# Half-height one-hots on two quarters of TensorE, and two of four banks summed on VectorE, in a three-layer GNN

## The chip, the cores and the metric

The kernel runs on one core of one Trainium2 chip. The metric is the device time of one execution in microseconds, the median over runs. All lines (L1404 and the like) are lines of the kernel before.

## The reference, cut to what matters

```python
h = jnp.maximum(_layernorm(x, axis=-1), 0.0)         # x: (12500, 64) fp32
for l in range(3):
    mlp = lambda z: jnp.maximum(z @ W1[l] + b1[l], 0.0) @ W2[l] + b2[l]
    msgs = mlp(h[dst])                               # 400,000 edges
    agg = segment_sum(msgs, src, num_segments=12500)
    h = mlp(h + agg)
return x + (h @ Wf + bf)
```

The edges are sorted by `dst`. Several edges may join the same two nodes.

## The kernel before, in words

**The idea.** Every layer sums the messages of the `dst` nodes into the `src` nodes over the same edges. So the kernel first builds a matrix of counts, "how many edges lead from this dst node to that src node", four bits a count, in DRAM (`counts_dram`). Each layer is then a dense product: message parts (`parts`, two fp16 halves that add up to the fp32 value) times unpacked counts (read as fp8), added up in PSUM. Layer 0 is in part multiplied while the matrix is still being built.

**Windows.** The nodes are handled as 49 tiles (`WT`) of 128 pairs of neighbouring dst nodes. The edges of a pair lie in one stretch of the sorted list. In the setup TensorE (L1336) and ScalarE (L1113, an activation with a sum) find for every pair where its stretch starts, in units of 16 edges (`GRAN`), in seven batches of seven tiles, and VectorE (L715 to L717) makes them the addresses `start_i`. The packing of edges into words (row key, column key, weight) is VectorE's L701 to L709 with a cast by GpSimd (L610). Per tile one indirect DMA of GpSimd (L621, `gather`) fetches 128 edges for each of the 128 pairs; six tiles are in flight (`WR`). ScalarE splits a tile's words (L1130, L1131), TensorE turns them so that edges lie on partitions (L1347, L1349), and ScalarE copies them to SBUF (`keep_keys`, L1139 to L1143).

**One-hots and the build.** A tile is done in four groups (`HG`) of 32 pairs. The loop over the 196 groups `k` is written out by hand on every engine, and each engine runs through its own list in order:
- VectorE's `make_hots(k)` compares keys with a row of numbers (both L754). Column one-hots `hot_c`: 26 two-byte words per pair, which hold 52 fp8 columns. Row one-hots `hot_r`: 128 per pair, 64 for each of its two dst nodes. From group 32 on ScalarE makes two of the 32 row one-hots (`find_few_distances` L1167, `make_few_rows` L1173), so that VectorE makes 30 (3840 elements). There are two slots: group k waits until the matmuls of group k-2 are done.
- GpSimd's `weigh(k)` (L636) multiplies the column one-hots by each edge's weight, as 416 words of 32 bits.
- TensorE's `multiply_group(k)` (L1375): one matmul per pair, all 128 edges by 128 rows (two nodes of 64) by 53 columns; the last column counts the edges. The result lies in two PSUM slots of 16 pairs.
- ScalarE's `keep_batch` (L1182, L1184) copies it out, VectorE's `turn_counts(k-2)` transposes it (L762), and SyncE stores it (L453).

**The rounds.** From tile 8 (`AHEAD`) on, TensorE does a part of layer 0 in every group, behind the build matmuls: `add_bank(u, b)`, with one unit `u` per tile and one bank `b` of four per group. A unit is 448 columns of a seventh of the nodes (`SB` = 7 stretches) and two chunks of seven tiles, so 14 matmuls of 448 columns (L1404). Seven units make a round over all stretches. From the second round on (unit 7, tile 15) the sums so far are first put back into the bank by a product with the identity in fp32 (`add_kept`, L1399), and after the 14 matmuls ScalarE copies the bank out again (`keep_sums`, L1191). Two banks of PSUM serve in turn. VectorE unpacks the counts for it, one pass a group (`unpack_low` L794, `unpack_high` L802), and makes `parts` where due (L843). SyncE loads the counts (L464).

The order on VectorE in group k, quoted in short, with L754, L762 and L794 or L802 in it:

```python
make_hots(k)                                   # columns, then rows
if k >= LAG: turn_counts(k - LAG)
if h == 0 and u >= 0: unpack_low(ROUND * u + 1)
if h == 1 and u >= 0: unpack_high(ROUND * u)
if h == 2 and u >= 0: unpack_high(ROUND * u + 1)
if h == 3 and 0 <= unit_of(j + 1) < FUSED: unpack_low(ROUND * unit_of(j + 1))
```

**Behind the build** eight units are left, then layers 1 and 2 (L1525, with the small matmuls L1481, L1487 and L1503 of the node network between the chunks).

## Time and profile before

| | |
|---|---|
| median of 3 runs | 2164.39 us (2163.72 to 2164.80) |
| the profiled execution | 2161.14 us |
| its span | 2159.4 us, mean granted clock of TensorE 0.979 |
| TensorE busy | 2025.7 us (94%), 15741 matmuls |
| VectorE busy | 1454.3 us (67%) |
| ScalarE busy | 793.6 us (37%) |
| GpSimd busy | 609.3 us (28%) |

The busy share of TensorE counts matmuls whose ends are modelled, so that neighbours overlap by a little; the distance from one start to the next is what a stream costs. The span falls into a setup (to 57.7 us), the build without rounds (to 194 us), the build with rounds (to 922 us), and the rest, in which TensorE has hardly any idle time. The page's slices show VectorE at nine tenths or more from slice 2 to slice 17 of 40, and at three to six tenths after them.

### The profile page before, as it was taken

What the parts mean: (1) busy time and instruction counts of PE and PEld (TensorE: products, weight loads), DVE (VectorE), ACT (ScalarE), POOL (GpSimd) and SP (SyncE); (2) the same over time, 40 slices, a digit from 0 to 9 for tenths busy, and PEclk for the clock granted to TensorE, in tenths of its full rate; (3) what the DMA queues carried; (4) which work ended last, traced back from release to release, by engine and by line L of the source; (5) the groups of instructions that cost most, each with busy time, mean ns of one, the idle gap of its engine ahead of it and who ended that gap; (6) DMA issues with size and microseconds to landing.
All of it is one profiled execution on the core that took longest, in us unless ns stands there. A gap on an engine that the chain in (4) does not pass through costs nothing.

```text
span 2159.4 us, 39820 instructions
## 1 busy us (share of the span) xinstructions
PE 2025.7 (94%) x15741; PEld 1138.4 (53%) x15741; DVE 1454.3 (67%) x1656; ACT 793.6 (37%) x2228; POOL 609.3 (28%) x273
## 2 busy tenths in 40 slices
PE   4565889999999999999999999999999999999998
PEld 3444445555565555555555555555555555555554
DVE  7999999999999999946643343343365444434433
ACT  4996887777777778722200000000010000000000
POOL 3666666666767666600000000000000000000000
PEclk8796999999999999999999999999999999999999
DMA  7356666666666666653444543543543555555452
GB/s 201 75 137 186 178 170 207 189 200 197 193 194 193 189 191 188 190 175 90 150 149 120 164 146 107 164 149 111 172 149 113 179 160 154 159 159 159 142 164 71
DMA packets 332829, 344.51 MB, mean 160 GB/s; under 512 B 21562, under 2 KB 303992, under 8 KB 332184
## 3 DMA queue, kind: packets, MB, share of 16 engines
q1 hardware_dynamic: 327516, 335.59, 52.6%
q0 software_dynamic: 2352, 6.43, 1.1%
q8 instruction: 94, 1.54, 0.3%
q10 hardware_dynamic: 2816, 0.53, 0.2%
q14 instruction: 51, 0.42, 0.1%
HBM read 252.58 MB, written 89.89 MB: 159 GB/s over the span
## 4 chain that ended last, share of the span: by engine, by line
PE 75%; DVE 15%; issue 3%; DMA 3%; ACT 2%; POOL 1%; SPq 1%; DVEq 0%; POOLq 0%; ACTq 0%
PE ps L1525 48%; PE ps L1404 15%; DVE arena L754 7%; PE ps L1375 4%; PE ps L1399 4%; DVE arena L762 3%; DMA arena<-counts_dram 2%; PE ps L1481 2%; PE ps L1503 1%; POOL arena L636 1%; PE ps L1487 1%; DVE arena L802 1%; SPq L453 1%; DVE arena L794 1%; ACT arena L1182 1%
## 5 line engine op out<-in xcount | busy, mean ns | idle before, releaser
L1525 PE MATMUL ps<-arena,parts 128*128 128x448 fp8e4 x5488 | 1049.1, 353 | 0.8 <-DVE arena L890 0.8
L1525 PEld LDWEIGHTS ps<-arena,parts 128*128 128x128 f16 x5488 | 534.7, 98 | 514.2 <-issue 24.6
L636 POOL TENSOR_TENSOR arena<-arena,weight_now 128x416 int32<-128x416 int32 x196 | 518.3, 2644 | 273.6 <-DVE arena L754 271.3
L877 DVE TENSOR_SCALAR arena<-arena 128x3136 uint16<-128x3136 uint16 x196 | 191.4, 976 | 592.2 <-PE ps L1525 592.2
L1404 PE MATMUL ps<-arena,parts 128*128 128x448 fp8e4 x2744 | 550.8, 353 | 1.5 <-DVE parts L843 1.5
L754 DVE TENSOR_TENSOR arena<-row_iota,key_now 128x3840 f16<-128x3840 f16 (+1 forms) x196 | 425.8, 2172 | 0.0
L1404 PEld LDWEIGHTS ps<-arena,parts 128*128 128x128 f16 x2744 | 266.4, 98 | 291.2 <-issue 73.1
L1274 ACT ACTIVATE arena<-arena 128x448 f32<-128x448 f32 x42 | 24.2, 577 | 988.9 <-DVE arena L904 988.9
L1182 ACT ACTIVATE arena<-ps 128x800 uint16<-128x800 f32 x392 | 338.4, 872 | 31.4 <-PE ps L1375 31.0
L1375 PE MATMUL ps<-arena 128*128 128x53 fp8e4 x6272 | 205.3, 189 | 76.6 <-POOL arena L636 64.1
L1375 PEld LDWEIGHTS ps<-arena 128*128 128x128 f16 x6272 | 195.6, 98 | 125.3 <-DVE arena L754 76.7
L762 DVE STREAM_TRANSPOSE arena<-arena 128x800 int32<-128x800 int32 x196 | 196.7, 1004 | 3.4 <-DMA counts_dram<-arena 3.4
L878 DVE TENSOR_SCALAR arena<-arena 128x3136 uint16<-128x3136 uint16 x196 | 190.2, 970 | 0.0
L627 POOL PARTITION_ALL_REDUCE scal<-scal x2 | 2.0, 1014 | 649.8 <-DVE scal L822 649.8
L649 POOL PARTITION_ALL_REDUCE good<-good x1 | 0.4, 409 | 565.4 <-DVE good L1031 565.4
L754 DVE TENSOR_TENSOR arena<-word_iota,key_now 128x832 uint16<-128x832 f16 x196 | 114.9, 586 | 0.0
L1167 ACT ACTIVATE few_far<-row_iota,few_now 128x128 f16<-128x128 f16 x328 | 112.1, 393 | 0.0
L794 DVE TENSOR_SCALAR arena<-arena 128x3136 uint16<-128x3136 uint16 x82 | 77.2, 942 | 5.0 <-DMA arena<-counts_dram 4.9
L621 POOL DMA_INDIRECT arena<-edges_dram,start_i x49 | 76.5, 1561 | 8.0 <-issue 5.4
L802 DVE TENSOR_SCALAR arena<-arena 128x3136 uint16<-128x3136 uint16 x82 | 76.6, 934 | 0.0
L1184 ACT ACTIVATE row_edges<-ps 128x16 f16<-128x16 f32 x392 | 75.6, 193 | 0.0
L1399 PE MATMUL ps<-msg,ident 128*128 128x448 f32 x140 | 68.9, 573 | 2.7 <-DVE arena L862 2.7
(150 smaller groups left out, 1176.7 us busy)
## 6 DMA issues: line engine op xcount, KB each, us to landing
arena<-counts_dram SPq DMA_DIRECT2D x294, 784.0 KB, 4.6
counts_dram<-arena SPq DMA_DIRECT2D x784, 100.0 KB, 2.2
h_dram<-parts SPq DMA_DIRECT2D x2, 1536.0 KB, 7.2
edges_dram<-arena SPq DMA_DIRECT2D x2, 1400.0 KB
arena<-in_x_dram SPq DMA_DIRECT2D x14, 192.0 KB
out_dram<-arena SPq DMA_DIRECT2D x14, 192.0 KB
arena<-in_dst_dram SPq DMA_DIRECT2D x1, 1400.0 KB
arena<-in_src_dram SPq DMA_DIRECT2D x1, 1400.0 KB
```

The source lines that it names most:

```text
L636: nc.gpsimd.tensor_tensor(pairs, pairs, weight_now[:, h * HW:(h + 1) * HW].unsqueeze(2).to_broadcast([P, HW, WORDS // 2]), ALU.mult).then_ ...
L754: return v.tensor_tensor(out, numbers.rearrange("p (m two) -> p m two", two=2).unsqueeze(1).to_broadcast(shape), key.unsqueeze(2).to_broad ...
L762: v.transpose(ctile[:, k % 2, :].bitcast(I32), stage[:, k % 2, :].bitcast(I32)).then_inc(s["counts_turned"], 1)
L794: v.tensor_scalar(spread[:, n % WIDE, 0, :].bitcast(U16), ring0[:, n % RING0, :].bitcast(U16), 0x0F0F, None, ALU.bitwise_and).then_inc(s[" ...
L877: v.tensor_scalar(spread[:, c % WIDE, 0, :].bitcast(U16), packed, 0x0F0F, None, ALU.bitwise_and)
L878: v.tensor_scalar(spread[:, c % WIDE, 1, :].bitcast(U16), packed, 4, 0x0F0F, ALU.logical_shift_right, ALU.bitwise_and).then_inc(s["counts_ ...
L1167: last = a.activation(few_far[:, c, :], row_iota[:], ACT.Abs, bias=few_now[:, k % HG, c:c + 1])
L1182: a.activation(to, product(q)[:, :, 0:2 * LP].rearrange("p c (m two) -> p c m two", two=2), ACT.Copy, scale=1.0 / WEIGHT_UNIT)
L1375: last = t.matmul(product(q)[:, c, 0:COLS], hot_r[:, slot, w, :], hot_c8[:, slot, w, 0:COLS], start=True, stop=True)
L1399: t.matmul(ps[:, bank, 0:NB], ident[:], kept_sums(u % SB, b), start=True, stop=False)
L1404: last = t.matmul(ps[:, bank, 0:NB], parts[:, (ROUND * (u // SB) + c) * CK + k, :], spread[:, c, b // 2, at:at + NB].bitcast(F8), start=(u ...
L1525: last = t.matmul(ps[:, b, 0:NB], parts[:, c * CK + k, :], spread[:, c % WIDE, b // 2, at:at + NB].bitcast(F8), start=start, stop=stop)
```

## The change

- A pair's two nodes get windows of their own: the partitions 0 to 63 hold 64 edges from the start of the first node, 64 to 127 hold 64 edges of the second (`REACH` = 64). The unit of a start is 8 edges instead of 16. There are two indirect DMAs per tile, of half the size each.
- The row one-hots of a pair are 64 wide instead of 128 (2048 elements per group), all on VectorE; ScalarE's part (L1141, L1167, L1173) goes.
- The column one-hots are fp16 instead of fp8: 50 words per pair instead of 26, and GpSimd multiplies 800 words of 32 bits.
- A pair takes two matmuls of 64 edges by 64 rows by 51 columns, on the quarters (rows 0 to 63, columns 0 to 63) and (64 to 127, 64 to 127) of the array.
- From unit 7 on, two of the four banks (`ADDED` = 0 and 2) are no longer put back by TensorE; VectorE adds the bank to the kept sums (`add_sums`), in the next group, between the transpose and the unpacking.
- The starts of 20 tiles are found in the setup, in five batches of four, with fp16 steps in two parts; those of the other 29 in the build, one tile each, seven tiles ahead (`node_step` and `find_starts` on VectorE, `make_fan_now` on TensorE, `count_fan_now` on ScalarE).
- The packing has fewer passes on VectorE; GpSimd's cast becomes a multiply and add. A small DMA of the next 64 entries of `dst` is put ahead of the load of `src` on SyncE's queue.

The diff, cut to its core:

```diff
-GRAN = 16
+GRAN = 8
+REACH = WIN // 2
+BATCH = 4
+BATCHES = 5
+FANS = BATCH * BATCHES
+FAN_AHEAD = 7
-FEW = 2
-FEW_FROM = 32
+ROWS = HROWS * HI
-WORDS = 2 * 13
+WORDS = 2 * LP
-COLS = 2 * WORDS + 1
+COLS = WORDS + 1
+ADDED = (0, 2)
...
-        hot_r, at = view(0, [SLOTS, HW, P], F16)
-        hot_c, at = view(at, [SLOTS, HW, CPITCH], F16)
+        hot_r, at = view(0, [SLOTS, HW, ROWS], F16)
+        hot_m, at = view(at, [SLOTS, HW, CPITCH], F16)
...
+        def sums_freed(u, b):
+            if u >= SB and b in ADDED:
+                return s["sums_added"], len(ADDED) * (u - SB) + ADDED.index(b) + 1
+            left = [n for n in range(SBB) if n not in ADDED]
+            if u >= SB:
+                return s["sums_kept"], SBB * SB + len(left) * (u - SB) + left.index(b) + 1
+            return s["sums_kept"], SBB * u + b + 1
...
@@ gpsimd, gather(t)
-                pool.indirect_dma_start(win[:, t % WR, :], None, edges_dram.rearrange("(r f) -> r f", f=2 * GRAN),
-                                        bass.IndirectOffsetOnAxis(ap=start_i[:, t:t + 1], axis=0)).then_inc(
-                    windows_gathered[t % WR], 16)
+                for d in range(2):
+                    pool.indirect_dma_start(win[:, t % WR, d * WIN:(d + 1) * WIN], None,
+                                            edges_dram.rearrange("(r f) -> r f", f=2 * GRAN),
+                                            bass.IndirectOffsetOnAxis(ap=start_i[:, t, d:d + 1], axis=0)).then_inc(
+                        windows_gathered[t % WR], 16)
@@ gpsimd, weigh(k)
-                pairs = hot_c[:, k % SLOTS, :, 0:WORDS].bitcast(I32)
+                pairs = hot_m[:, k % SLOTS, :, 0:WORDS].bitcast(I32)
@@ vector, packing of the edges, per half
-                v.tensor_scalar(e1[:, c], src_t[:, c], 3, None, ALU.bitwise_and)
-                link(v.tensor_scalar(e2[:, c], src_t[:, c], 4, None, ALU.bitwise_and), dve)
-                link(v.tensor_scalar(e2[:, c].bitcast(F32), e2[:, c], 32.0 * 255 / 4, 32.0, ALU.mult, ALU.add), dve)
+                link(v.tensor_scalar(e1[:, c], src_t[:, c], 3, None, ALU.bitwise_and), dve)
...
-                v.scalar_tensor_tensor(pk_weight[:, units, :], by_units(e1)[:, units, :], 0.25,
-                                       by_units(e2.bitcast(F32))[:, units, :], ALU.add, ALU.mult).then_inc(s["edges_packed"], 1)
+                v.tensor_scalar(pk_weight[:, units, :], by_units(e1)[:, units, :], 4096.0, 15360.0, ALU.mult,
+                                ALU.add).then_inc(s["edges_packed"], 1)
@@ vector, make_hots(k)
-                few = FEW if k >= FEW_FROM else 0
-                compare_keys(hot_r[:, slot, few:HW, :].rearrange("p c (m two) -> p c m two", two=2), row_iota[:], P,
-                             key_now[:, u, 0, w.start + few:w.stop, :]).then_inc(s["rows_made"], 1)
+                compare_keys(hot_r[:, slot, :, :].rearrange("p c (m two) -> p c m two", two=2), row_iota[:], ROWS,
+                             key_now[:, u, 0, w, :]).then_inc(s["rows_made"], 1)
@@ vector
+            def add_sums(u, b, bank):
+                dve.wait_ge(s["sums_done"], SBB * u + b + 1)
+                dve.wait_ge(*sums_freed(u - SB, b))
+                kept = kept_sums(u % SB, b)
+                v.scalar_tensor_tensor(kept, ps[:, bank, 0:NB], scal[:, 0, 6:7], kept, ALU.mult, ALU.add).then_inc(
+                    s["sums_added"], 1)
@@ vector, in the loop over k, behind turn_counts
+                before = unit_of((k - 1) // HG)
+                if before >= SB and (k - 1) % HG in ADDED:
+                    add_sums(before, (k - 1) % HG, (k - 1) % 2)
@@ vector, in the loop over k, behind the unpacking
+                if fan_of(j) >= 0 and h == 0:
+                    node_step(fan_of(j))
+                if fan_of(j) >= 0 and h == 3:
+                    find_starts(fan_of(j), 1)
@@ scalar, setup: per tile two passes of 408 in place of one of 200
+            def count_fan(t, frm, scrap):
+                for d in range(2):
+                    a.activation(scrap[:, d, :], frm[:, 0:FANX], ACT.Sign, scale=-1.0, bias=node_less[:, d, t:t + 1],
+                                 accum_out=signs[:, t, d:d + 1])
@@ scalar, in the loop over k
-                if k and unit_of((k - 1) // HG) >= 0:
-                    b = (k - 1) % HG
-                    keep_sums(unit_of((k - 1) // HG), b, b % 2)
-                if FEW_FROM <= k + 1 < BUILD * HG:
-                    find_few_distances(k + 1)
+                before = unit_of((k - 1) // HG)
+                if before >= 0 and ((k - 1) % HG not in ADDED or before < SB):
+                    keep_sums(before, (k - 1) % HG, (k - 1) % 2)
...
+                if fan_of(j) >= 0 and h == 2:
+                    count_fan_now(fan_of(j))
@@ tensor, multiply_group(k)
-                        last = t.matmul(product(q)[:, c, 0:COLS], hot_r[:, slot, w, :], hot_c8[:, slot, w, 0:COLS], start=True,
-                                        stop=True)
+                        for d in (slice(0, REACH), slice(REACH, WIN)):
+                            last = t.matmul(product(q)[d, c, 0:COLS], hot_r[d, slot, w, :], hot_m[d, slot, w, 0:COLS],
+                                            start=True, stop=True)
@@ tensor, add_bank(u, b)
-                    pe.wait_ge(s["sums_kept"], SBB * u + b - 1)
+                    pe.wait_ge(*sums_freed(*divmod(SBB * u + b - 2, SBB)))
...
-                if u >= SB:
+                if u >= SB and b not in ADDED:
+                    pe.wait_ge(*sums_freed(u - SB, b))
                     add_kept(u, b, b % 2)
@@ tensor, in the loop over k
+                if h == 1 and fan_of(j) >= 0:
+                    make_fan_now(fan_of(j))
```

## Rows read from the trace of the kernel before

**Rows 1.** The page, the chain that ended last, by line
```profile
PE ps L1525 48%; PE ps L1404 15%; DVE arena L754 7%; PE ps L1375 4%; PE ps L1399 4%; DVE arena L762 3%; DMA arena<-counts_dram 2%; PE ps L1481 2%; PE ps L1503 1%; POOL arena L636 1%; PE ps L1487 1%; DVE arena L802 1%; SPq L453 1%; DVE arena L794 1%; ACT arena L1182 1%
```

**Rows 2.** Windows over L754: us, busy DVE (instructions), clock, DMA share, GB/s
```profile
57.60:194.40 136.80, 89.87 (x64) 0.77 0.49 126
194.40:326.70 132.30, 74.21 (x56) 0.96 0.63 182
326.70:918.40 591.70, 357.76 (x270) 1.00 0.66 193
```

**Rows 3.** Timeline of one group: start us, us, engine, line, what [idle before]
```profile
602.51 1.71 POOL L621 DMA_INDIRECT arena<-edges_dram,start_i  x1
...
602.81 1.00 PE L1375 MATMUL ps<-arena 128*128 128x53 fp8e4 x32
...
603.30 0.57 DVE L754 TENSOR_TENSOR arena<-word_iota,key_now 128x832 uint16<-128x832 f16 x1
...
603.64 1.00 PE L1399 MATMUL ps<-arena,ident 128*128 128x448 f32 x2
603.81 2.14 DVE L754 TENSOR_TENSOR arena<-row_iota,key_now 128x3840 f16<-128x3840 f16 x1
...
604.24 2.48 POOL L636 TENSOR_TENSOR arena<-arena,weight_now 128x416 int32<-128x416 int32 x1
...
604.48 2.81 PE L1404 MATMUL ps<-arena,parts 128*128 128x448 fp8e4 x14
...
605.88 0.99 DVE L762 STREAM_TRANSPOSE arena<-arena 128x800 int32<-128x800 int32 x1
606.80 0.92 DVE L794 TENSOR_SCALAR arena<-arena 128x3136 uint16<-128x3136 uint16 x1
...
607.13 1.00 PE L1375 MATMUL ps<-arena 128*128 128x53 fp8e4 x32
...
607.66 0.57 DVE L754 TENSOR_TENSOR arena<-word_iota,key_now 128x832 uint16<-128x832 f16 x1
```

**Rows 4.** Timeline, the first group of the build, VectorE and GpSimd
```profile
58.18 2.29 DVE L754 TENSOR_TENSOR arena<-row_iota,key_now 128x4096 f16<-128x4096 f16 x1
58.42 2.81 POOL L636 TENSOR_TENSOR arena<-arena,weight_now 128x416 int32<-128x416 int32 x1 [5.40 <-DVE arena L754]
60.38 1.29 DVE L754 TENSOR_TENSOR arena<-word_iota,key_now 128x832 uint16<-128x832 f16 x1
```

**Rows 5.** Lines by form: row one-hots; busy us, mean ns, idle before
```profile
L754 DVE TENSOR_TENSOR arena<-row_iota,key_now 128x3840 f16<-128x3840 f16 x164 | 352.7, 2151 | 0.0
...
L754 DVE TENSOR_TENSOR arena<-row_iota,key_now 128x4096 f16<-128x4096 f16 x32 | 73.0, 2282 | 0.0
```

**Rows 6.** Lines by form: a bank read with one kept operand
```profile
L890 DVE SCALAR_TENSOR_TENSOR arena<-ps,scal,msg 128x448 f32<-128x448 f32 x14 | 9.5, 681 | 3.9 <-PE ps L1404 3.9
```

**Rows 7.** Lines by form: fp32 weight loads of 128 and of 64 columns
```profile
L1487 PEld LDWEIGHTS ps<-arena,W1b 128*128 128x128 f32 x56 | 10.6, 190 | 6.5 <-issue 5.2
...
L1481 PEld LDWEIGHTS ps<-arena,W1s 128*64 128x64 f32 x168 | 8.8, 135 | 16.4 <-issue 15.8 <-DVE arena L893 0.7
```

**Rows 8.** Timeline of TensorE in a later layer
```profile
1052.44 0.97 PE L1481 MATMUL ps<-arena,W1s 128*64 128x448 f32 x4
1053.35 5.47 PE L1525 MATMUL ps<-arena,parts 128*128 128x448 fp8e4 x28
...
1064.96 1.67 PE L1487 MATMUL ps<-arena,W1b 128*128 128x448 f32 x4
1066.46 10.76 PE L1525 MATMUL ps<-arena,parts 128*128 128x448 fp8e4 x56
```

**Rows 9.** Timeline of VectorE in the setup, one small link
```profile
38.74 0.17 DVE L717 TENSOR_SCALAR start_i<-start_f 128x7 int32<-128x7 f32 x1
```

**Rows 10.** Lines by form: setup on ScalarE and VectorE
```profile
L1113 ACT ACTIVATE row_edges<-ps,node_less 128x200 f16<-128x200 f32 x49 | 20.4, 465 | 1.2 <-PE ps L1336 1.2
...
L709 DVE SCALAR_TENSOR_TENSOR arena<-arena 125x1600 f16<-125x1600 int32 x2 | 3.6, 1818 | 0.0
```

More of the change, by code:

```diff
@@ L695, in _ @@
+            for n in range(BATCHES):
                 node_steps(n)
@@ L722, in _ @@
+            for n in range(2):
+                find_starts(n * BATCH, BATCH)
             less, var, inv, tmp = (stat[:, j, :] for j in range(4))
@@ L728, in _ @@
                 if t.start == 0:
-                    for n in range(3, 5):
-                        find_starts(n)
+                    for n in range(2, 4):
+                        find_starts(n * BATCH, BATCH)
             link(last, dve)
@@ L738, in _ @@
             v.tensor_tensor(less, counted[:, 1, 0, :], counted[:, 1, 1, :], ALU.add)
-            for n in range(5, GROUPS):
-                find_starts(n)
+            for n in range(4, BATCHES):
+                find_starts(n * BATCH, BATCH)
             dve.wait_ge(s["root_made"], 1)
@@ L1264, in _ @@
                     keep_weights()
-            keep_sums(FUSED - 1, SBB - 1, (SBB - 1) % 2)
-            for b in range(SBB):
-                keep_sums(FUSED, b, b)
+            for u, b in [(FUSED - 1, SBB - 1)] + [(FUSED, b) for b in range(SBB)]:
+                if b not in ADDED:
+                    keep_sums(u, b, b if u == FUSED else b % 2)
             def epilogue(l, i):
@@ L1326, in _, with make_fan @@
             pe.wait_ge(s["shift_made"], 1)
-            pe.wait_ge(s["firsts_made"], 1)
-            t.matmul(ps[0:EP, 0, 0:FAN], shift, firsts, start=True, stop=True).then_inc(s["firsts_shifted"], 1)
+            pe.wait_ge(s["lasts_made"], 1)
+            t.matmul(ps[0:EP, 0, 0:FANX + 1], shift, lasts[:, 0:FANX + 1], start=True, stop=True).then_inc(s["lasts_shifted"], 1)
             pe.wait_ge(s["rises_made"], 1)
-            for n in range(GROUPS):
+            def make_fan(to, steps):
+                for part in range(2):
+                    last = t.matmul(to, steps, rises[:, part, 0:FANX + 1], start=part == 0, stop=part == 1)
+                return last
+            for n in range(BATCHES):
                 pe.wait_ge(s["steps_made"], n + 1)
```

245 lines of the change are left out of this document (139 added, 106 removed).

## The prediction

> **What bounds the kernel now.** I read the chain that ended last first, for the lines that set the end. It gives 48% to the matmuls of the later layers (L1525), 15% to those of the build's rounds (L1404), and 7% to the one-hots of VectorE (L754) [rows 1]. The change leaves L1525 alone, so the question is the build, whose stages the windows over L754 show [rows 2]: 32 groups (64 one-hots, two per group) in 136.8 us before the rounds begin, 28 in 132.3 us in the rounds that add nothing kept, 135 in 591.7 us after them, or 4.38 us a group. That last stage decides.
>
> One group in order of time [rows 3] shows two engines full at once. **VectorE**, start to start: column one-hots 0.51, row one-hots 2.07, transpose 0.92, unpack 0.86; 4.36 us. **TensorE**: 32 build matmuls 0.83, the kept sum brought back as fp32 0.84, 14 matmuls of the round 2.65; 4.32 us. A third resource hides in the same rows. GpSimd's multiplication (L636) starts at 604.24, 0.43 into VectorE's row one-hots, and ends at 606.72, 0.77 after they end (605.95), inside the transpose. That looks like a wait, not like work. In the one place without a transpose behind [rows 4] the row one-hots end at 60.47 and GpSimd's end is 61.23; the next column one-hots, 0.58 us long with nothing in their way, take 1.29. So each of the two holds the other up: the multiplication itself is 0.71 to 0.76 us, say 0.72, of exclusive time for 416 elements, and the transpose hides it.
>
> **The change, part by part** (136 groups from tile 15 on, in pairs, since every second bank is treated another way).
>
> *VectorE's one-hots.* Rows go from 3840 to 2048 elements. 4096 against 3840 elements is 2282 against 2151 ns [rows 5], 0.51 ns each, so 2.07 becomes 1.15. Columns go from 832 to 1600 elements of the same two bytes: 0.51 becomes 0.90. Together 2.58 becomes 2.05.
>
> *GpSimd's multiplication* grows from 416 to 800 elements. In proportion to 0.72 that is 1.38 us of exclusive time [rows 4]; below, it could be as little as 0.72, were it all fixed, and above I see no row. I take 1.38, as no fixed part shows. The transpose (0.92) no longer covers it, so VectorE waits 0.46 for its unpack, unless an add stands there too.
>
> *The adds on VectorE.* Two banks of four become a read of a bank with one kept operand, the form of L890, 0.68 us long [rows 6], 0.60 start to start. A group with one: 2.05 + 0.92 + 0.60 + 0.86 = 4.43. One without: 2.05 + 1.38 + 0.86 = 4.29. This alone is 8.72 a pair against 8.76 now: what the one-hots save, the lock and the adds take back. But an add also waits for its bank. The multiplication of group k ends 3.43 after the group began on VectorE and 0.17 pass until a load; then come X (the build matmuls), 2.65, 0.16 for the last matmul's end (2.81 in place of 2.65 [rows 3]), the add 0.60 and the unpack 0.86 before group k+2 can start: 7.9 + X a pair.
>
> *TensorE.* Two kept sums of four go: 0.84 less in a pair. The 32 build matmuls of 128 rows by 53 columns become 64 of 64 rows by 51 columns, on two opposite quarters. This is X, and no row shows it. From below: both quarters work at once and a pair costs what one costs now, 0.83 us a group. From above: a load of 64 columns and its matmul per quarter, one after another. Loads of 64 and 128 fp32 columns are 135 and 190 ns [rows 7]; 55 ns for 64 columns, times 64, is 3.5 us. In the middle: the present rate, one load and matmul in 26 ns (0.83 / 32), is a rate of issue, and 64 give 1.67; or both quarters load at once at 55 ns, 32 x 55 = 1.76. Two of my routes meet there, so I take 1.67. Going to another division of the array and back costs too: four passes of L1481 on two halves take 0.91 to the next matmul, four of L1487 on the whole array 1.50 [rows 8]. At full overlap the former would be 0.75, so the two changes cost 0.16, and they come in every group: X = 1.83.
> The Trainium skill (TensorEngine Tiling (Array Packing), Key Properties) says that tiles load and multiply in parallel and that changing the mode drains the engine; the L1481 rows agree with both, for 448 columns.
> The Trainium skill (TensorE: Matmul & The Clock Gate, Weight-path perf modes and LDWEIGHTS) speaks against the change: the fast load needs all 128 columns and goes off with column tiling, and a plain load costs the columns over 1.2 GHz, 53 ns for 64. By that X is 1.7 if the loads overlap and 3.4 if they don't.
>
> A pair on TensorE is then 2 x (1.83 + 2.65) + 0.84 = 9.80, and VectorE's loop 7.9 + 1.83 = 9.73. TensorE leads. A tile of four groups adds about 0.17 for turning keys, which lay beside VectorE before: 19.8.
>
> *Fans in the rounds.* 29 of 49 tiles (20 to 48) get their window starts in the build, in tiles 13 to 41. TensorE: two matmuls of 409 columns, near 2.65 / 14 = 0.19 each, 0.35 a tile with loads. VectorE: three small links of 0.17 [rows 9] and a step, 0.65 a tile. ScalarE: about 1.5 us in a tile, covered, as it loses the near-row helpers (L1167, L1173) and half of the kept copies. So tiles 15 to 41 take 20.15 against 17.53 (4 x 4.38): 27 x 2.62 = +71. Tiles 42 to 48: 7 x 2.27 = +16.
>
> *Tiles 8 to 14.* TensorE 1.83 + 2.65 + 0.04 = 4.52, VectorE 4.29 and 0.6 for parts in every second group, as before: 0. ScalarE keeps all banks here.
>
> *Before the rounds.* A group is 2.05 + 1.38 = 3.43, against 3.63 (0.51 + 2.20 [rows 4] + 0.92); where a message follows (13 groups), it runs in GpSimd's time and saves the 0.46 more. That is -12. GpSimd issues a second gather per tile: 1.71 [rows 3], so two outlast the 2.1 free before its next multiplication by about 1 us in eight tiles, +8. If the multiplication then misses its gap it waits a whole one-hot, which I count in the range.
>
> *Setup.* VectorE drops two passes over 1600 elements in each half and its 1.82 us pass L709 [rows 10] has one source; at half of 1.82 for a one-source pass, 2 x 2.7 = -5. ScalarE's counting: 40 passes of 408 in place of 49 of 200, 465 ns each [rows 10]; 20 us becomes some 24, beside the stores of the edges. The load of dst's next 64 entries stands ahead of src on SP's queue, at well under 1 us. Twelve gathers against six, at most 1.71 each, come ahead of the first multiplication; they start earlier by what the packing saves. I take -5 for all. The drain behind the build loses two kept sums: -1.
>
> **Sum**: +71 + 16 + 0 - 4 - 5 - 1 = +77 on the profiled execution's 2161.1, which is 2238; the median of the runs is 3.3 above it, 2241.5. Everything behind the build is untouched.
>
> **Rivals.**
> *Quarters at once* (X = 0.99 with the mode changes). For it: L1481 ran its halves together. Against: those matmuls are eight times as long as these, so issue never showed. VectorE's loop then leads: 8.9 a pair and 0.5 a tile, 18.3 against 17.53: +21 in tiles 15 to 41, +2 behind, -2 in tiles 8 to 14, -10 before: 2176. Slower in spite of it.
> *Faster: the lock is cheap.* X = 0.99, and GpSimd's multiplication is mostly fixed cost, so that the transpose still covers it. It decides on the unpack's start behind the transpose: below 0.92 us of exclusive time VectorE pays nothing. A pair is then 3.83 + 4.43 = 8.26 and its loop 8.4, so tiles 15 to 41 17.3 (-6), 42 to 48 16.8 (-5), tiles 8 to 14 28 x 0.5 (-13), before them -13, setup and end -6: 2121, and between that and 2176 for a lock between 0.92 and 1.38.
> *Loads one after another*, X = 3.66: a pair on TensorE 13.5, a tile 27.5: +270 and +68, +46 in tiles 8 to 14, +30 before: 2565. For it: nothing in the trace shows two loads together. Against: nothing shows them held apart. The Trainium skill's rule on the fast load, without overlap, gives the same.
> *The change does nothing*: excluded, since the shapes change on every engine.
>
> **Numbers.** Forecast 0.42, quarters at once 0.25, faster 0.20, loads in turn 0.13. The range leaves out the loads in turn and the low end of the faster case: 2125 to 2275, which takes X from 0.9 to 2.0. A measurement of this kernel tells about 0.2% (4.3 us) from no change. Faster 0.22 (0.02 from the quarters case), same 0.06, slower 0.72.
>
> **What would show it.** Right: in the rounds TensorE without idle time, 64 build matmuls in 1.6 to 1.9 us, groups of 4.9 to 5.1 us; VectorE waiting for L1404 ahead of its adds; L636 still ending in or just behind the transpose, now with 1.4 us behind the row one-hots. Wrong: build matmuls of a group under 1.2 us (then read VectorE's unpack: late by 0.46 or not), or over 2.5 us; an L636 that ends 0.9 us or less behind the row one-hots; a setup that moves by over 10 us.

## The result, and the profile after

The changed kernel (span of the profiled execution 2209.8 us) takes **2214.8 us** (median, 2211.7 to 2215.8) against 2164.6 in the same call: ratio **1.0227, 95% interval 1.0209 to 1.0244**, 50 us slower. The forecast was 2241.5. Direction and range held; the size was 27 us too large, on a forecast excess of 77.

First the page, its chain that ended last, by engine and by line.

```profile
PE 88%; issue 4%; DVE 3%; ACT 2%; DMA 2%; POOL 1%; SPq 0%; DVEq 0%; POOLq 0%; ACTq 0%
PE ps L1618 47%; PE ps L1494 24%; PE ps L1465 9%; PE ps L1489 3%; PE ps L1574 2%; PE ps L1596 1%; DVE arena L822 1%; PE ps L1580 1%; DMA arena<-in_src_dram 1%; POOL arena L674 1%; POOL arena L690 1%; ACT parts L1218 1%; ACT arena L1260 1%; PE ps L1409 0%; DMA edges_dram<-arena 0%
```

L1618 is the old L1525, L1494 the old L1404, L1465 the build matmul (old L1375), L1489 the kept sum (old L1399) [rows 1]. VectorE's one-hots have left the chain (7% to 1%), and it looks as if TensorE bounded the build. It doesn't, as the timeline shows. Next the stages, windows over the one-hots (L822, old L754), which answer to [rows 2]; columns as there.

```profile
54.40:193.60 139.20, 74.64 (x65) 0.77 0.50 127
193.60:324.00 130.40, 59.22 (x57) 0.96 0.66 189
324.00:965.70 641.70, 285.94 (x271) 1.00 0.63 178
```

The 50 us lie in the last row, 641.7 us in place of 591.7. The first group starts 3.2 us earlier, groups 0 to 31 take 2.4 more, tiles 8 to 14 1.9 less. Within the last row, tiles 15 to 41, which now also make window starts, go from 17.55 to 19.19 us each (27 tiles, +44), and the groups of tiles 42 to 48 from 4.37 to 4.57 (+6). What is behind the last group grew by 3 us. That is not TensorE's work: the rounds that are left end 1.5 us sooner than before, and the layers behind them take the same. 4.4 us stand at the very end, from VectorE's last operation to the end of the span (4.7 us before, 9.0 now), where GpSimd's last instruction, a drain, takes 8.15 us in place of 4.07. All the changed kernels have it (8.6 to 9.0 us); why is not shown.

Now the timeline of the changed kernel over one of the tiles with a fan, VectorE, TensorE and GpSimd only (start, us, engine, line, operation, and in brackets the idle time before it). It starts with the third group of a tile.

```profile
601.72 0.98 DVE L822 TENSOR_TENSOR arena<-word_iota,key_now 128x1600 uint16<-128x1600 f16 x1
...
602.17 0.52 PE L1409 MATMUL ps<-arena 125*128 125x409 f16 x2
...
602.52 0.92 PE L1489 MATMUL ps<-msg,ident 128*128 128x448 f32 x2
602.62 1.22 DVE L822 TENSOR_TENSOR arena<-row_iota,key_now 128x2048 f16<-128x2048 f16 x1
602.85 2.39 POOL L690 TENSOR_TENSOR arena<-arena,weight_now 128x800 int32<-128x800 int32 x1 [2.08 <-DVE arena L822]
...
603.27 2.81 PE L1494 MATMUL ps<-arena,parts 128*128 128x448 fp8e4 x14
...
603.75 1.00 DVE L830 STREAM_TRANSPOSE arena<-arena 128x800 int32<-128x800 int32 x1
604.68 1.39 DVE L869 TENSOR_SCALAR arena<-arena 128x3136 uint16<-128x3136 uint16 x1
...
606.01 1.19 PE L1465 MATMUL ps<-arena 64*64 64x51 f16 x64
...
608.94 1.55 POOL L690 TENSOR_TENSOR arena<-arena,weight_now 128x800 int32<-128x800 int32 x1
610.00 0.68 DVE L1042 SCALAR_TENSOR_TENSOR arena<-ps,scal,arena 128x448 f32<-128x448 f32 x1 [0.97 <-PE ps L1494]
...
610.60 0.97 DVE L861 TENSOR_SCALAR arena<-arena 128x3136 uint16<-128x3136 uint16 x1
...
611.95 0.99 DVE L822 TENSOR_TENSOR arena<-word_iota,key_now 128x1600 uint16<-128x1600 f16 x1
...
613.09 2.39 POOL L690 TENSOR_TENSOR arena<-arena,weight_now 128x800 int32<-128x800 int32 x1 [2.60 <-DVE arena L822]
...
615.58 1.19 PE L1465 MATMUL ps<-arena 64*64 64x51 f16 x64 [0.20 <-issue]
...
616.71 2.82 PE L1494 MATMUL ps<-arena,parts 128*128 128x448 fp8e4 x14
...
619.57 0.68 DVE L1042 SCALAR_TENSOR_TENSOR msg<-ps,scal,msg 128x448 f32<-128x448 f32 x1
...
621.05 0.98 DVE L822 TENSOR_TENSOR arena<-word_iota,key_now 128x1600 uint16<-128x1600 f16 x1
```

Four readings.

**X is 1.13 us**: from the build matmuls at 615.58 to the round at 616.71, not 1.83.

**The lock is as forecast** (the lock: GpSimd's multiplication and VectorE's operations hold each other up, and what they can't share is the multiplication's exclusive time). The row one-hots end at 603.84, GpSimd's multiplication at 605.24, 1.40 later (forecast 1.38). The transpose covers 0.93 of it and the unpack L869 lasts 1.39 in place of some 0.97.

**A loop leads, not TensorE.** A pair of groups is 9.10 us where nothing comes between. The one that starts at 611.95 ends at 621.05: multiplication's end 3.53, build 0.10 later, X 1.13, round and its last end 2.86, add 0.60, unpack 0.88, in all 9.10. TensorE idles before the build (0.20 there; 0.63 before the one at 610.59). The trace puts that down to "issue", but the build at 615.58 starts 0.10 behind the multiplication's end at 615.48: it is GpSimd's product that it waits for.

**The other pair takes 10.23** (601.72 to 611.95), 1.13 more: find_starts adds 0.47 on VectorE before the next group, and the build at 606.01 starts 0.77 behind the multiplication instead of 0.10, as TensorE is still in the round of 603.27, which came late behind keys turned, the fan (L1409) and a kept sum. 9.10 + 10.23 = 19.33 for this tile, against the stage's mean of 19.19. Over tiles 15 to 41 the two pairs take 9.10 and 10.09 on average, and the build of a tile's third group starts 0.63 behind its multiplication, that of the other three 0.10.

So I had three causes to test: that the quarters work at once, the loop through the add, and the lock. The question behind them is which of these the 50 us are.

### The profile page after: what moved, and what is told of

Its sections match the earlier page's. It is cut to its first block, busy times and chain, and to the rows that moved or that the text cites. A ratio compares the mean times of both kernels' runs of the same rounds, so it can differ in the third digit from the quotient of the medians.

```text
span 2209.8 us, 51883 instructions
## 1 busy us (share of the span) xinstructions
PE 2048.1 (93%) x21873; PEld 1148.9 (52%) x21873; DVE 1454.7 (66%) x1835; ACT 660.3 (30%) x1693; POOL 587.2 (27%) x326
## 4 chain that ended last, share of the span: by engine, by line
PE 88%; issue 4%; DVE 3%; ACT 2%; DMA 2%; POOL 1%; SPq 0%; DVEq 0%; POOLq 0%; ACTq 0%
PE ps L1618 47%; PE ps L1494 24%; PE ps L1465 9%; PE ps L1489 3%; PE ps L1574 2%; PE ps L1596 1%; DVE arena L822 1%; PE ps L1580 1%; DMA arena<-in_src_dram 1%; POOL arena L674 1%; POOL arena L690 1%; ACT parts L1218 1%; ACT arena L1260 1%; PE ps L1409 0%; DMA edges_dram<-arena 0%
## 5 line engine op out<-in xcount | busy, mean ns | idle before, releaser
L1618 PE MATMUL ps<-arena,parts 128*128 128x448 fp8e4 x5488 | 1049.1, 353 | 1.1 <-DVE arena L957 1.1
L1618 PEld LDWEIGHTS ps<-arena,parts 128*128 128x128 f16 x5488 | 534.7, 98 | 514.5 <-issue 24.9
L944 DVE TENSOR_SCALAR arena<-arena 128x3136 uint16<-128x3136 uint16 x196 | 191.3, 976 | 592.4 <-PE ps L1618 592.4
L1494 PE MATMUL ps<-arena,parts 128*128 128x448 fp8e4 x2744 | 552.3, 354 | 2.6 <-issue 2.5
L690 POOL TENSOR_TENSOR arena<-arena,weight_now 128x800 int32<-128x800 int32 x196 | 431.5, 2202 | 327.6 <-DVE arena L822 326.9
L1494 PEld LDWEIGHTS ps<-arena,parts 128*128 128x128 f16 x2744 | 260.9, 98 | 264.6 <-issue 45.0
L1465 PE MATMUL ps<-arena 64*64 64x51 f16 x12544 | 245.8, 191 | 100.1 <-issue 66.1
L1465 PEld LDWEIGHTS ps<-arena 64*64 64x64 f16 x12544 | 228.5, 113 | 176.0 <-issue 175.3
L822 DVE TENSOR_TENSOR arena<-row_iota,key_now 128x2048 f16<-128x2048 f16 x196 | 238.0, 1214 | 0.0
L822 DVE TENSOR_TENSOR arena<-word_iota,key_now 128x1600 uint16<-128x1600 f16 x196 | 199.5, 1018 | 5.9 <-PE ps L1465 5.9
L945 DVE TENSOR_SCALAR arena<-arena 128x3136 uint16<-128x3136 uint16 x196 | 190.0, 970 | 0.0
L674 POOL DMA_INDIRECT arena<-edges_dram,start_i x98 | 143.0, 1459 | 22.9 <-issue 11.1
L861 DVE TENSOR_SCALAR arena<-arena 128x3136 uint16<-128x3136 uint16 x82 | 99.8, 1217 | 2.8 <-DMA arena<-counts_dram 2.8
L869 DVE TENSOR_SCALAR arena<-arena 128x3136 uint16<-128x3136 uint16 x82 | 99.4, 1212 | 0.0
L1302 ACT ACTIVATE parts<-msg,scal 128x448 f16<-128x448 f32 x42 | 25.8, 668 | 100.6 <-DVE msg L982 57.0
L960 DVE TENSOR_SCALAR arena<-ps,scal 128x448 f32<-128x448 f32 x56 | 38.1, 682 | 24.8 <-PE ps L1618 24.6
```

The costliest lines, as they stand in the source:

```text
L674: pool.indirect_dma_start(win[:, t % WR, d * WIN:(d + 1) * WIN], None, edges_dram.rearrange("(r f) -> r f", f=2 * GRAN), bass.IndirectOffs ...
L690: nc.gpsimd.tensor_tensor(pairs, pairs, weight_now[:, h * HW:(h + 1) * HW].unsqueeze(2).to_broadcast([P, HW, WORDS // 2]), ALU.mult).then_ ...
L822: return v.tensor_tensor(out, numbers.rearrange("p (m two) -> p m two", two=2).unsqueeze(1).to_broadcast(shape), key.unsqueeze(2).to_broad ...
L861: v.tensor_scalar(spread[:, n % WIDE, 0, :].bitcast(U16), ring0[:, n % RING0, :].bitcast(U16), 0x0F0F, None, ALU.bitwise_and).then_inc(s[" ...
L869: v.tensor_scalar(spread[:, n % WIDE, 1, :].bitcast(U16), ring0[:, n % RING0, :].bitcast(U16), 4, 0x0F0F, ALU.logical_shift_right, ALU.bit ...
L944: v.tensor_scalar(spread[:, c % WIDE, 0, :].bitcast(U16), packed, 0x0F0F, None, ALU.bitwise_and)
```

## Experiments

All times are medians; the kernel before was run beside each set (2164.7, 2165.7 and 2164.0 in the three sets). "Tile" is the mean of tiles 15 to 41, "group" that of tiles 42 to 48, between starts of the column one-hots. Stages are those of the profiled execution. Ratios are to the kernel before, with 95% intervals.

| kernel | us | ratio | groups 0–31 | tiles 8–14 | tile | group |
|---|---|---|---|---|---|---|
| before | 2164.6 | 1 | 136.7 | 132.3 | 17.55 | 4.37 |
| after | 2214.8 | 1.0227 [1.0209, 1.0244] | 139.2 | 130.4 | 19.19 | 4.57 |
| quarters in turn | 2291.7 | 1.0591 [1.0569, 1.0612] | 160.1 | 134.4 | 20.72 | 5.01 |
| no adds | 2222.5 | 1.0271 [1.0253, 1.0289] | 137.7 | 131.1 | 19.26 | 4.64 |
| half weighed | 2172.9 | 1.0033 [1.0020, 1.0047] | 137.2 | 125.5 | 18.22 | 4.35 |
| late adds | 2208.1 | 1.0207 [1.0190, 1.0225] | 142.1 | 131.1 | 19.02 | 4.38 |
| split gathers | 2220.3 | 1.0252 [1.0235, 1.0269] | 140.7 | 129.6 | 19.44 | 4.55 |
| late adds, split gathers | 2179.4 | 1.0064 [1.0047, 1.0081] | 139.2 | 129.8 | 18.13 | 4.34 |
| late adds, split gathers, starts first | 2199.0 | 1.0155 [1.0138, 1.0172] | 141.9 | 129.8 | 18.85 | 4.34 |
| late, split, starts first, half weighed | 2169.7 | 1.0021 [1.0009, 1.0032] | 136.6 | 121.1 | 18.11 | 4.26 |
| late, split, half weighed | 2157.5 | 0.9968 [0.9956, 0.9980] | 134.4 | 123.6 | 17.82 | 4.30 |
| late, split, gaps used | 2175.5 | 1.0046 [1.0034, 1.0058] | 141.2 | 129.4 | 17.98 | 4.36 |
| late, split, four added | 2184.5 | 1.0094 [1.0079, 1.0109] | 138.1 | 129.7 | 18.40 | 4.41 |

### Do the quarters work at once?

```diff
-                    for c in range(QW):
-                        w = q % 2 * QW + c
-                        for d in (slice(0, REACH), slice(REACH, WIN)):
+                    for d in (slice(0, REACH), slice(REACH, WIN)):
+                        for c in range(QW):
+                            w = q % 2 * QW + c
```

The same 64 matmuls, but 16 on one quarter and then 16 on the other.

> Same 64 build matmuls of a group, but 16 on one quarter, then 16 on the other, and again, instead of alternating. In the changed kernel 64 take 1.13 us to the next matmul, mode changes of 0.16 us included: 15 ns each. If this rate comes from two quarters working at once, in turn each needs 30 ns or more: 2.1 us a group or above, the loop 10.0 us a pair: 2275 us or more (with loads of 53 ns that nothing overlaps, 3.5 us a group and 2450 us). If it is a rate of issue of 15 ns each, nothing changes: 2210 to 2220 us.

Measured 2291.7. The timeline of this kernel:

```profile
955.00 2.82 PE L1494 MATMUL ps<-arena,parts 128*128 128x448 fp8e4 x14
...
957.75 1.90 PE L1465 MATMUL ps<-arena 64*64 64x51 f16 x64
959.59 0.23 PE L1438 MATMUL ps<-ident,rk_now 128*128 128x128 f16 x1
```

In turn the 64 take 1.84 us, alternating 1.13. The starts of the single matmuls in the two traces say more than these sums. In turn they are 27 ns apart on average; alternating 16, two on opposite quarters 3 to 4 ns apart and then 28 to 29 to the next two. From the last of the 64 to the next matmul it is 0.12 us in both kernels, against 0.03 before the change. So alternating quarters overlap, though not fully: 1.7 times the rate, not 2. One quarter alone keeps about the rate of the whole array before (26 ns).

The changes of division come out of the same starts: 0.09 us behind the build, and 0.09 ahead of it (2.75 from the round at 955.00 to the build at 957.75, 2.65 before). That is 0.19 a group, for which the forecast had 0.16, but only half of it lies in X.

Early on, in a stretch of granted clock 0.50 (the 1.2 GHz level), X is 2.95 (63.08 to 66.03) in turn against 1.84 (62.45 to 64.29). And 1.84 at the full clock is my X of 1.83: this kernel is the one that I had forecast, with tiles of 20.72 and groups of 5.01 where I said 20.15 and 4.95. It takes 2291.7, though, and not 2241.5. With its own X the forecast is 50 us too low and out of its range: 27 of them in groups 0 to 31 (+23 us where I said -4), 15 in tiles 15 to 41.

### Is it the adds, or the lock?

```diff
-ADDED = (0, 2)
+ADDED = ()
```

> ADDED is empty: TensorE puts every bank back and ScalarE copies every bank out, as before the change; one-hots, quarters, gathers and fans stay. Theory L: no add, no loop; TensorE leads with 2 x (1.13 + 2.65 + 0.84) = 9.25 us a pair and 19.1 us a tile, without idle time: about the same time as the changed kernel, 2213 us (2205 to 2222). Rival P (TensorE already the bound at 19.2 us a tile): 0.84 more in each pair, 2272 us. Rival G (only VectorE with GpSimd's exclusive time counts): 17.9 us a tile, 2170 us.

Measured 2222.5, just above the range expected: without the adds it is 8 us slower still, with groups of 4.64 where the sum of TensorE's own work said 4.62. By stages, the rounds of tiles 15 to 48 take 3 us more (645.1 for 641.7) and what is behind the last group 7, where TensorE still puts back kept sums that VectorE added before (13 matmuls of L1489 for 6). The adds as such are not the loss; VectorE's adds cost no more than the kept sums that TensorE is spared.

```diff
-                pairs = hot_m[:, k % SLOTS, :, 0:WORDS].bitcast(I32)
+                pairs = hot_m[:, k % SLOTS, :, 0:24].bitcast(I32)
```

(the weight's broadcast is cut to 12 in the same way)

> GpSimd multiplies 384 of the 800 words of a group; the other columns keep their one-hots unweighted, so this part of the counts is left out. Theory L with an exclusive multiplication (1.38 us for 800 words, 0.66 for 384): the unpack behind the transpose is 0.97 us again in place of 1.39, the multiplication ends 0.7 us earlier, a pair's loop falls from 9.0 to 8.3, TensorE leads with 17.4 us a tile: 2145 us (2135 to 2165). Rival P: no change, 2210 to 2218. If the multiplication were mostly fixed cost, it would end at the same distance behind the row one-hots (1.4 us) and the time stay at 2215.

Measured 2172.9, 42 us back, short of the 2145 expected (2135 to 2165). Lines of the last stage for this kernel (its first three rows), then for the changed kernel.

```profile
L690 POOL TENSOR_TENSOR arena<-arena,weight_now 128x384 int32<-128x384 int32 x135 | 205.4, 1522 | 294.1 <-DVE arena L822 234.1 <-ACT weight_now L1237 59.6
...
L869 DVE TENSOR_SCALAR arena<-arena 128x3136 uint16<-128x3136 uint16 x68 | 64.6, 950 | 0.0
L861 DVE TENSOR_SCALAR arena<-arena 128x3136 uint16<-128x3136 uint16 x66 | 63.0, 954 | 3.4 <-DMA arena<-counts_dram 3.3
```

```profile
L690 POOL TENSOR_TENSOR arena<-arena,weight_now 128x800 int32<-128x800 int32 x135 | 299.2, 2216 | 239.8 <-DVE arena L822 239.3
...
L869 DVE TENSOR_SCALAR arena<-arena 128x3136 uint16<-128x3136 uint16 x68 | 80.0, 1177 | 0.0
```

The multiplication now ends 0.71 us behind the row one-hots (603.75 against 603.04), and the unpack, 950 instead of 1177 ns, waits for nothing. From 384 to 800 elements the exclusive time goes from 0.71 to 1.40 us: 1.66 ns for each further element, and hardly a fixed part (1.66 x 384 is 0.64 of the 0.71). That was the assumption of the forecast. But the multiplication stands in the loop as well, so this run shortens both, and can't tell them apart. The next ones can.

### Taking the loop away

```diff
-                before = unit_of((k - 1) // HG)
-                if before >= SB and (k - 1) % HG in ADDED:
-                    add_sums(before, (k - 1) % HG, (k - 1) % 2)
+                before = unit_of((k - 2) // HG)
+                if before >= SB and (k - 2) % HG in ADDED:
+                    add_sums(before, (k - 2) % HG, (k - 2) % 2)
```

VectorE adds a bank one group later, when its round is long done (the last one moves behind the loop).

> VectorE adds the bank of group k-2 instead of k-1, at the same place of its list, so that the bank has long been finished. Reference is the changed kernel: 2214.8 us, 19.2 us a tile in tiles 15 to 41, 4.57 us a group behind them. Theory L (a loop: one-hots, multiplication, build, round, add, unpack, two groups long, 7.9 + 1.13 = 9.0 us a pair and more where TensorE is late): the wait of the adds for L1494 goes, VectorE and the exclusive time of GpSimd are left, 18.2 us a tile and 4.36 us a group: 2182 us (2175 to 2190). Rival P (TensorE's issue of 128 small instructions in a group is the bound, as the chain with 88% TensorE has it): no change, 2210 to 2218.

Measured 2208.1, outside the range expected (2175 to 2190). The groups of tiles 42 to 48 do what the loop theory says, 4.38 from 4.57. The tiles hardly move, 19.02. The timeline of this kernel tells why.

```profile
606.81 1.65 POOL L674 DMA_INDIRECT arena<-edges_dram,start_i  x1 [0.16 <-issue]
...
608.45 1.22 DVE L822 TENSOR_TENSOR arena<-row_iota,key_now 128x2048 f16<-128x2048 f16 x1
...
608.77 1.71 POOL L674 DMA_INDIRECT arena<-edges_dram,start_i  x1 [0.30 <-DVE arena L822]
...
610.50 1.55 POOL L690 TENSOR_TENSOR arena<-arena,weight_now 128x800 int32<-128x800 int32 x1
610.51 2.38 DVE L861 TENSOR_SCALAR arena<-arena 128x3136 uint16<-128x3136 uint16 x1
```

The change issues two gathers in a row. The second ends at 610.48, while the column one-hots that the multiplication waits for were done when the row one-hots began, at 608.45. The multiplication starts at 610.50 in place of some 608.7, loses the time of the transpose, and the unpack pays for it: 2.38 us instead of 1.39. In the changed kernel the same two gathers stand at 605.39 and 607.21 and delay it to 608.94, but there VectorE waits for its bank until 610.00 anyway. With the loop gone the next wait came up. So I issued one gather behind each of two multiplications:

```diff
-                for d in range(2):
+                for d in halves_of:
...
-                if k % HG == 2 and k // HG + WR < WT:
-                    gather(k // HG + WR)
+                if k % HG in (0, 2) and k // HG + WR < WT:
+                    gather(k // HG + WR, (k % HG // 2,))
```

> The late adds, and the two gathers of a tile apart: one behind the multiplication of the tile's first group, one behind that of its third. With late adds alone the third and fourth group took 4.4 and 5.7 us: two gathers of 1.7 us end 0.8 us after the row one-hots, the multiplication comes late, and the unpack (2.38 us in place of 0.97) is held up for its whole length. If that is what the late adds alone left over, the long unpack goes and a tile takes 17.44 + 0.75 = 18.2 us: 2180 us (2172 to 2188). Rival: the gathers cost nothing, the 0.8 us of a tile are fans and turning of keys on TensorE: 2205 to 2210.

> The changed kernel with the gathers apart, adds where the change has them. Theory L: in the rounds the loop over the add's wait leads whether the gathers are early or not (in the tile read, VectorE stands 0.97 us before its add while TensorE finishes L1494): at most 0.2 us a tile, and a few us before the rounds: 2208 us (2203 to 2215). Rival: the gathers alone make the changed kernel slow, 2180 us.

Both edits together: 2179.4, as expected, 35 us of the 50 back. The gathers alone: 2220.3, above the 2208 expected (2203 to 2215). That is no gain; the 5.5 us more than in the changed kernel are hardly clear of the spread (the two intervals overlap). As long as the loop leads, the late multiplication is free. Late adds alone gave 7, so the two are worth 35 only as a pair.

### What is left: VectorE, and the lock

With both edits VectorE runs without waiting for TensorE (group starts at 600.57, 604.85, 609.25, 613.99 and 618.60). Each group is its own work plus the lock. With GpSimd's work halved on top:

> Late adds and split gathers as in the run at 2179, and GpSimd multiplies 384 of the 800 words of a group's column one-hots, so that 416 words a group keep no weight (the output is that of other weights); the start rows are found where they were, so nothing waits for ScalarE's sum. Lock theory: VectorE's unpack no longer waits for GpSimd (0.42 us in groups without an add). The early groups go as in the other half-weigh runs, 2.6 us less in groups 0 to 31 and 8.7 in groups 32 to 59; in the rounds VectorE drops below TensorE, which then leads at 4.26 us a group (tiles 42 to 48 of the run that had both) plus some 0.65 a fan tile, 17.7 against 18.13 us a tile, 11.6 over 27 tiles, and 2.2 in tiles 42 to 48: 2179 - 25 = 2154 us (2145 to 2163). Rival, that the lock costs nothing once nothing waits elsewhere: 2174 to 2182.

Measured 2157.5: 22 us less, and 0.3% faster than the kernel before, though with the output of other weights. Windows over L822 of this kernel, to be read against the ones of the changed kernel:

```profile
53.92:188.35 134.43, 67.21 (x65) 0.80 0.51 132
188.35:311.94 123.59, 59.26 (x57) 0.97 0.67 193
311.94:909.30 597.36, 285.53 (x271) 1.00 0.66 192
```

As late adds and split gathers alone give 139.2, 129.8 and 606.9 us there, halving GpSimd's work gives back 4.8, 6.2 and 9.5. Two groups of a tile without an add pay 0.42 of lock each, 23 us over tiles 15 to 41, and only 8 of them come back there. The groups show why: a tile's second group falls from 4.28 to 3.82, but the first and third, which issue a gather, grow by 0.23 each.

```profile
600.78 0.64 DVE L1042 SCALAR_TENSOR_TENSOR arena<-ps,scal,arena 128x448 f32<-128x448 f32 x1
600.79 0.97 POOL L674 DMA_INDIRECT arena<-edges_dram,start_i  x1
601.34 1.20 DVE L861 TENSOR_SCALAR arena<-arena 128x3136 uint16<-128x3136 uint16 x1
```

The multiplication ends sooner, so that the gather now starts ahead of the unpack and holds it up, 1.20 us instead of 0.96; with the whole multiplication it started behind the unpack and waited itself (1.65 us instead of 0.97). So a gather takes part in the lock too. In tiles 42 to 48, without gathers, TensorE leads: 2 x (1.13 + 2.74) + 0.84 = 8.58 a pair, 4.29 a group, measured 4.30. The 22 us can't be had for the real output, whose 800 elements all need their weight.

The other side of the same claim: where an add stands between transpose and unpack, it should cost only what it exceeds the wait by. All four banks added:

```diff
-ADDED = (0, 2)
+ADDED = (0, 1, 2, 3)
```

> All of the computation; late adds and split gathers as in the run at 2179, and VectorE adds up all four banks instead of two. The add (0.60 us) stands between the transpose and the unpack, where the unpack otherwise waits 0.42 us for GpSimd's weighing. Lock theory: an add in these groups costs 0.60 - 0.42 = 0.14 to 0.18 us in place of 0.60, and 68 such groups from tile 15 on give 10 to 12 us: 2179 + 11 = 2190 us (2183 to 2195). If the wait for GpSimd isn't what the gap is, the add costs its 0.60 in full: 2179 + 41 = 2220 us. TensorE loses a kept matmul in these groups, so it doesn't come up.

Measured 2184.5, the group 4.41 for 4.34 and the tile 18.40 for 18.13. Half of the groups get an add that they hadn't, so it costs them 0.14 us each and not 0.60 (from its start to the unpack's it is 0.56 here, less the wait of 0.42). The gap behind the transpose is GpSimd's.

### Filling the gap

If that gap is idle anyway, the small operations of the fan could stand in it. The first try put find_starts ahead of the unpack in the last group of the tile, with and without the halved multiplication.

> Late adds, gathers apart, and the three links of find_starts ahead of the unpack, in the time in which GpSimd holds VectorE up anyway (0.46 us). A tile 17.7 us in tiles 15 to 41, as before the change (17.55); with 4.38 us a group behind and a few us more in setup and drain: 2167 us (2160 to 2175), the same as before within 0.3%. Rival: the links don't fit there (they need ScalarE's sum of the group before): 2180 us.

> The same with 384 of 800 words multiplied, which leaves the weights of the other columns out. What is left is VectorE's own work, 2 x 3.84 + 2 x 4.44 + 0.5 = 17.1 us a tile, and TensorE's, 4 x 3.78 + 1.69 + 0.6 = 17.4: 2145 us (2135 to 2155), clearly below the kernel before. If instead the exclusive time of GpSimd doesn't count once adds and gathers are out of the way, the same as the run without it, 2167.

Measured 2199.0 and 2169.7, where 2167 and 2145 were expected: both worse than without the move (2179.4 and 2157.5). The timeline of the former:

```profile
605.14 1.00 DVE L830 STREAM_TRANSPOSE arena<-arena 128x800 int32<-128x800 int32 x1
607.27 0.16 DVE L781 SCALAR_TENSOR_TENSOR start_f<-signs,rows_before 128x2 f32<-128x2 f32 x1 [1.14 <-ACT rows_before L1213]
```

VectorE waits 1.14 us for ScalarE's counts, which were ready in time one unpack later. The second try takes them from the tile before, in its second group, makes the fan's step in the fourth group ahead of the unpack, and puts the gathers behind groups 1 and 3:

```diff
+                if h == 1 and fan_of(j - 1) >= 0:
+                    find_starts(fan_of(j - 1), 1)
+                if h == 3 and fan_of(j + 1) >= 0:
+                    node_step(fan_of(j + 1))
```

> All of the computation. Late adds; one gather behind the weighing of group 1 of a tile, the other behind that of group 3; the start rows of a tile are found one group pair later, in group 1 of the next tile ahead of the unpack (0.47 us of VectorE in the 0.42 us in which the unpack would wait for GpSimd, and ScalarE's sum is long there), and the step one-hot of the fan (0.19 us) is made in group 3 ahead of the unpack. If VectorE sets the pace of tiles 15 to 41 by its own work plus the lock, 0.42 + 0.19 = 0.6 us a tile go, 17.5 against 18.13, and 27 tiles give 16 us: 2163 us (2158 to 2170), level with the kernel before. Rival, that TensorE's path (4.26 us a group and the fan's 0.65, 17.7 a tile) comes up at once: 2168. Rival, that these small operations are not hidden or that a new wait takes their place: 2177 or more.

Measured 2175.5, the best version that computes everything, but 12 us short of what I expected. Its timeline:

```profile
602.31 0.57 DVE L781 SCALAR_TENSOR_TENSOR start_f<-signs,rows_before 128x2 f32<-128x2 f32 x1
602.91 0.17 DVE L783 TENSOR_SCALAR start_f<-start_f 128x2 f32<-128x2 f32 x1
603.11 0.17 DVE L784 TENSOR_SCALAR start_i<-start_f 128x2 int32<-128x2 f32 x1
603.19 0.97 DVE L869 TENSOR_SCALAR arena<-arena 128x3136 uint16<-128x3136 uint16 x1
...
611.44 0.64 DVE L757 TENSOR_SCALAR arena<-arena 125x128 f16<-125x128 f32 x1
612.01 0.96 DVE L861 TENSOR_SCALAR arena<-arena 128x3136 uint16<-128x3136 uint16 x1
```

The small operations are held up themselves: over the tiles of this stage L781 lasts 0.57 instead of 0.15 us and L757 0.64 instead of 0.28. What follows the wait is not covered either: from the end of L781 (602.88) to the unpack (603.19) there are 0.31 us for two more links. The tile's second group takes 4.73 for the 4.28 without them, 0.45 more, which is all of find_starts. VectorE's transpose and add are not held up: they last 1.00 and 0.64 wherever the multiplication stands, and that is why four adds fitted in and three links don't. Only 0.15 us a tile came of the move.

## Why the prediction was right in direction and off in size

- **The step that failed is the size of X** ("Two of my routes meet there, so I take 1.67") and what was built on it, "TensorE leads". X is 1.13, not 1.83. A pair on TensorE is then 2 x (1.13 + 2.65) + 0.84 = 8.40 (8.58 with the change into the quarters), and the loop 7.87 + 1.13 = 9.00 (measured 9.10): the loop leads, as in the rival *Quarters at once*. I had taken 26 ns for a rate of issue; the loads of fp32 columns and the present rate met by accident. The trace before could have told: the two halves of L1481 start 6 to 7 ns apart (1052.441 and 1052.447 us), loads and matmuls alike, so issue did show there, contrary to what I wrote against the rival.
- **The size was close in part by luck.** X too large made the forecast 77 us too high (what X of 1.84 in place of 1.13 costs in the runs: 2291.7 against 2214.8), and all the rest made it 50 too low. 27 is what the two leave.
- **That rival was right in mechanism and short in sum**: it said 2176, 39 us too low. In tiles 15 to 41 it had 18.3 a tile, the runs show 19.19. It left out that TensorE's keys, fan and kept sum make the next build late, by 0.67 us in the tile read (0.77 for 0.10) and 0.53 on average, in one of a tile's two pairs, and it took X 0.14 too small in each of them: 0.8 of the 0.9 us a tile. The groups 0 to 31 and the setup gave -1 where it had -10 (the drain's -1 among them), tiles 42 to 48 +6 for +2, and the end +3 where nothing was expected. My own forecast had +71 in tiles 15 to 41, +16 in tiles 42 to 48 and 0 in tiles 8 to 14; measured +44, +6 and -2.
- **One-hots: right.** 0.90 and 1.13 us, start to start, for the forecast's 0.90 and 1.15 (2.03 for 2.05).
- **Lock: right.** 1.40 us for 1.38, the unpack's wait 0.42 for 0.46, and in proportion to the elements. Halving it gives back 22 us once the loop is gone, 8 of them in tiles 15 to 41, where the gathers take up most of the room.
- **Add: right**, 0.60 (0.56 behind the transpose), and so was the form of the loop (7.9 + X a pair).
- **Gathers: half seen.** I counted two gathers as late only before the rounds (+8). In the rounds they are late as well; it is hidden while the loop leads, and costs 29 us when it doesn't (2208.1 to 2179.4).
- **Groups 0 to 31** took +2.4 for the forecast's -4. In turn they took 23.4 more than before, so I had been wrong to give X no weight in a stage where TensorE runs at a mean granted clock of 0.77. The waits of VectorE in this stage, changed kernel first, then the kernel before (its L781 and L1394 are the new L848 and L1484):

```profile
DVE msg L848 <- PE ps L1484: 11.4, 7, 3.3
DVE arena L822 <- PE ps L1465: 5.9, 1, 5.9
```
```profile
DVE msg L781 <- PE ps L1394: 2.9, 1, 2.9
```

So VectorE's own work fell by the 12 us forecast, but it waits 17.9 us in place of 2.9: seven times for TensorE's message matmuls, and once for the first build (VectorE's third group starts only at 64.46), as the first multiplication stands behind the gathers, at 60.75. I had +8 for waits. Behind the last group I had -1, and the rounds did end 1.5 us sooner; the 4.4 us of the program's end had no term at all.

- **The Trainium skill's rule** (TensorE: Matmul & The Clock Gate, LDWEIGHTS (loading the stationary operand)), a plain load at 53 ns for 64 columns, gave X 1.7 with overlap and 3.4 without. The runs show 1.13 and 1.84, and 27 ns for a load with its matmul on one quarter, so no load of 53 ns stands between these matmuls. That the fast load goes off with column tiling, which I put to the same page, stands in the Trainium skill's TensorEngine Tiling (Array Packing), Restrictions; no run here shows it. The Trainium skill's other rule (TensorEngine Tiling (Array Packing), Key Properties), that tiles load and multiply in parallel, the trace bears out: 1.13 against 1.84 us by the order alone.

**Where the 50 us went.** Together, not by one cause: 35 are the two waits, the loop through the add and the gathers behind it, and neither comes off without the other. The remaining 15 are the rounds again; in the other stages gains and losses cancel, the 4.4 us of the program's end among them. In the rounds it is the change's own balance on VectorE. It saves 0.55 us of one-hots in a group and pays 0.42 of lock in groups without an add or 0.60 in groups with one, and some 0.65 of fan work a tile: 0.5 us a tile by this sum, 0.58 measured. Even at its best (2175.5) it is 0.5% behind the kernel before.

## What to carry to other kernels

When work is moved from one engine to another, write down the loop that it closes (here multiplication, build, round, add, unpack, the group after next) beside the sums of each engine; the longest of these leads, and moving the consumer back by one group takes the loop away (here it cost nothing by itself). Two waits that hide each other have to be removed together, or each looks worthless. And where VectorE and GpSimd hold each other up, an operation of VectorE that is not held up costs little in that time (0.14 us of its 0.60), if it needs nothing that is late; one that is held up itself gains nothing there. Which is which was read here from durations: the transpose and the add keep theirs, the unpack and the small links don't. Last, look at the starts of single matmuls before you take a mean distance for a rate of issue.

## What the runs showed of the hardware

- Matmuls of 64 x 64 by 51 columns, each with its own load, start 16 ns apart on average when opposite quarters alternate (3 to 4 ns within two, 28 to 29 to the next two) and 27 ns apart when one quarter takes 16 in a row, at a granted clock of 1.00. The kernel before has 26 ns for 128 x 128 by 53 columns.
- Going from the whole array to the quarters and back costs 0.09 us each way, 0.19 a group: 0.28 us from a round's last matmul to the build in place of 0.19, and 0.12 from the build's last to the next in place of 0.03.
- GpSimd's multiplication of 32-bit elements costs 1.66 ns of exclusive time for each further element (0.71 us for 384, 1.40 us for 800), with hardly a fixed part. Its duration in the profile is 2.39 us where it starts in VectorE's row one-hots and 1.55 where it starts behind them (608.94), so 2.39 includes time in which VectorE keeps it out.
- The wait on VectorE's side is charged to the first operation that is held up: an unpack of 0.97 us reads 1.39 and, behind the late multiplication, 2.38; a link of 0.15 reads 0.57. The transpose (1.00) and the add out of PSUM (0.64) are not lengthened.
- GpSimd's issue of an indirect DMA is in the same lock: 0.97 us with no unpack in its way and 1.65 behind one, and an unpack behind it takes 1.20 in place of 0.96.
